# First batch of the last attention, begun inside the feed-forward

## Chip, cores, metric

One core of one Trainium2 chip. The metric is the device time of the whole kernel in microseconds (us), lower is better.

## What is computed

A two-layer stack on x of shape (4, 512, 256), with a context of (4, 64, 256). All data are fp32.

```python
x = x + xattn0(layernorm(x), ctx)      # 12 heads of 64, layernorms of q and k
x = x + ffn0(layernorm(x))
x = x + xattn1(layernorm(x), ctx, mask)  # 16 heads of 16, 64 keys, masked softmax
x = x + moe(layernorm(x))              # 8 experts, top 1

def ffn0(x):   # 256 -> 1024 -> 1024 -> 1024 -> 256, ternary weights, scales per output
    h = silu((x @ w1.T) * s1) * ((x @ w2.T) * s2)
    h = gelu((h @ h1.T) * t1)
    h = gelu((h @ h2.T) * t2)
    return (h @ w3.T) * s3

def xattn1(q, k, v, mask):
    scores = (q @ Wq.T + bq) . (k @ Wk.T + bk) / 4, where(mask == 0, -1e9)
    return softmax(scores) . (v @ Wv.T + bv) @ Wo.T + bo
```

## The kernel before

The core runs four stages in a row: first attention, feed-forward, last attention, experts. Each of the first three loops over the four batches of 512 tokens (four token tiles of 128). The program for each engine is written out by hand, in the order in which its instructions stand, and semaphores tie the engines together. An engine that waits holds everything that stands behind the wait in its own program. PSUM has eight banks of 128 x 512 fp32: the feed-forward turns through banks 2 to 7 (`ring_bank`, L1086), banks 0 and 1 are for transposes, queries, probabilities and heads.

**Feed-forward** (`ffn_tensor` L1158, `ffn_scalar` L1249, `ffn_vector` L1264, `ffn_gpsimd` L1140). The hidden values are kept transposed, 128 hidden units by 512 tokens, as a rounded part and a remainder (`f_ha`, `f_hb`: `hi` and `lo`), since the ternary weights are exact in the one-pass form of fp32. So each product is a sum of matmuls for `hi` and for `lo`. Per batch there are four layers. The first has eight columns of two products each (`fw1`, `fw2`): ScalarE takes Silu of the one into `f_raw`, VectorE multiplies it by the other (L1273), rounds it (L1279) and takes the remainder (L1280). The second (`fh1`) and third (`fh2`) have eight products of 16 matmuls of 128x512, ScalarE takes Gelu, VectorE splits the result in the same way. `f_raw` has three buffers, so ScalarE waits for the split of three results before. The fourth layer (`fw3`) gives four token products, one for each token tile, of 16 matmuls of 256 columns. Its first two are issued as a pair. VectorE's end of a token tile (from L1292) is: product times scale into `f_tmp`, sum with the residual, moments, variance plus epsilon.

In batch 0, VectorE also checks the bits of the weights of the third and fourth layers, between the first and the second layer's splits (L1281), and sends TensorE a flag (`take_bits`, `f_checked`); TensorE reads it before the last product of the second layer. Both forms of every product stand in the program, behind a branch, and the one-pass form is what runs with these weights.

**Last attention** (`attn1_tensor` L1528, `attn1_scalar` L1688, `attn1_vector` L1777, `attn1_gpsimd` L1434, `attn1_sync` L1364). For batch b: columns are the transposed normalised tokens (`attn1_columns` L1303, copied out by ScalarE, L1338); queries are their product with `Wq` (L1331, copied out with scale and bias, L1343); both go through banks 0 and 1. Keys are spread over head blocks by GpSimd (`attn1_keys` L1423). The scores of a token tile (L1543, L1547) are ten matmuls into two banks, 2 and 3 or 4 and 5 in turn. VectorE takes the maximum over each head's 64 keys and subtracts it (L1787, L1788), ScalarE takes the exponential, VectorE the sum and its reciprocal (L1796, L1797), GpSimd divides (L1456). TensorE transposes the probabilities (L1562), multiplies them by the values (`heads`, L1572), projects (L1586). The gate part (L1318) is a product of the columns with the experts' gate weights, and `fold` (L1595, L1599) folds `Wo` and its bias into the gate weights, once.

Before the change, the first batch's columns and queries stand in the feed-forward's third layer of the last batch (after its fourth and sixth product, L1231 to L1235), and everything else of the attention stands behind the feed-forward. TensorE's order for batch b of the attention (L1643): scores of tiles 0 and 1, gate part, columns of batch b+1, queries of batch b+1, scores of tile 2, scores of tile 3, with the transposes, heads and projections of earlier batches between them; batch 0 has `fold` last. Scores of tile n in all wait for the subtraction two tiles before. SyncE loads the second-layer weights of all experts (8 MB, `ew2`) after the first batch's fourth scores (L1367).

## Time and profile before

| | us |
|---|---|
| median of three runs | 800.45 |
| lowest, highest | 796.26, 801.01 |
| the profiled execution | 798.0 |
| span of its instructions | 796.1 |
| TensorE busy in the span | 745.0 |
| VectorE busy | 460.0 |
| ScalarE busy | 248.4 |
| GpSimd busy | 183.4 |

The profile shows one execution. PE is TensorE, DVE is VectorE, ACT is ScalarE, POOL is GpSimd, SP is SyncE. PEclk is the granted clock of TensorE as a share of full speed. A timeline's row is a run of equal instructions: its start, its length, and in brackets how long the engine stood idle before it and on whom it waited.

### The profile page before, as it was taken

To read this page: it belongs to the slowest core of one execution; us is meant where nothing else is said; L and a number is where in the kernel's file an instruction comes from. 1 tells how busy PE (TensorE), PEld (TensorE's weight loads), DVE (VectorE), ACT (ScalarE), POOL (GpSimd) and SP (SyncE) were. 2 spreads that over 40 slices of the span, in tenths; PEclk is the share of its full clock that TensorE was granted. 3 is DMA by queue.
4 is the path that set the end of the run, shared out by engine and by line. 5 is a ranking of instruction groups with operands and counts; after the bars stand their busy time and mean duration, and the time that the engine had idled before them with its cause. 6 is when DMAs were issued, how large, how long until landed. Compare 5 with 4: busy or idle time off the path is not lost.

```text
span 796.1 us, 11304 instructions
## 1 busy us (share of the span) xinstructions
PE 745.0 (94%) x4168; PEld 578.6 (73%) x4168; DVE 460.0 (58%) x897; ACT 248.4 (31%) x455; POOL 183.4 (23%) x183
## 2 busy tenths in 40 slices
PE   5999899989999999999999999998987699999995
PEld 3676576768878888888888888775554597777674
DVE  4646479888982584348424943289798742333331
ACT  3425133132311132123222321256566232223221
POOL 3012134461020002000200020056564222222221
PEclk9979999999999999999999999999999899999998
DMA  9970800002300000000000000019013878899950
GB/s 326 383 254 2 369 1 0 1 1 80 134 2 2 2 2 2 2 2 2 2 2 2 2 2 2 2 25 412 1 54 107 275 268 312 259 282 302 310 159 7
DMA packets 21726, 86.64 MB, mean 109 GB/s; under 512 B 3229, under 2 KB 12384, under 8 KB 16352
## 3 DMA queue, kind: packets, MB, share of 16 engines
q1 hardware_dynamic: 19088, 78.18, 27.8%
q0 software_dynamic: 2560, 7.34, 2.7%
q8 instruction: 59, 0.97, 0.5%
q14 instruction: 19, 0.16, 0.1%
HBM read 79.22 MB, written 18.35 MB: 123 GB/s over the span
## 4 chain that ended last, share of the span: by engine, by line
PE 79%; DVE 13%; issue 4%; DMA 1%; ACT 1%; POOL 1%; SPq 0%; DVEq 0%; POOLq 0%
PE ps L1178 37%; PE ps L2177 8%; PE ps L2150 6%; PE ps L593 5%; PE ps L544 4%; PE ps L2142 3%; PE ps L1331 2%; PE ps L530 2%; DVE any_bits L357 2%; DVE head_max L1787 1%; PE ps L622 1%; DVE head_sum L1796 1%; PE ps L538 1%; DMA xs<-rows,token_in 1%; PE ps L1543 1%
## 5 line engine op out<-in xcount | busy, mean ns | idle before, releaser
L1256 ACT ACTIVATE f_raw<-ps,cols 128x512 f32<-128x512 f32 x96 | 66.2, 690 | 242.1 <-PE ps L1178 219.4
L1178 PE MATMUL ps<-f_ha_hi,fh 128*128 128x512 f32 x256 | 99.9, 390 | 1.6 <-DVE inexact L377 1.5
L1178 PE MATMUL ps<-f_hb_hi,fh 128*128 128x512 f32 x256 | 100.1, 391 | 0.0
L1178 PE MATMUL ps<-f_ha_lo,fh 128*128 128x512 f32 x256 | 99.6, 389 | 0.0
L1178 PE MATMUL ps<-f_hb_lo,fh 128*128 128x512 f32 x256 | 99.6, 389 | 0.0
L1279 DVE CAST f_ha_hi<-f_raw 128x512 fp32r<-128x512 f32 x64 | 27.6, 432 | 84.9 <-ACT f_raw L1256 83.9
L2177 PE MATMUL ps<-ew,hT 128*128 (+1 forms) x320 | 72.7, 381 | 2.3 <-ACT hT L2230 1.8
L2177 PEld LDWEIGHTS ps<-ew,hT 128*128 128x128 f32 (+1 forms) x320 | 52.5, 169 | 16.5 <-issue 4.4
L1178 PEld LDWEIGHTS ps<-f_ha_hi,fh 128*128 128x128 f32 x256 | 48.1, 188 | 12.3 <-issue 2.4
L1178 PEld LDWEIGHTS ps<-f_hb_lo,fh 128*128 128x128 f32 x256 | 48.1, 188 | 10.2 <-issue 0.2
L1178 PEld LDWEIGHTS ps<-f_hb_hi,fh 128*128 128x128 f32 x256 | 48.1, 188 | 10.2 <-issue 0.2
L1178 PEld LDWEIGHTS ps<-f_ha_lo,fh 128*128 128x128 f32 x256 | 48.1, 188 | 9.9
L2150 PE MATMUL ps<-xsT,ew 128*128 128x128 f32 (+1 forms) x416 | 50.4, 281 | 1.5 <-DVE xsT L2019 1.5
L2150 PEld LDWEIGHTS ps<-xsT,ew 128*128 128x128 f32 x416 | 49.6, 197 | 2.6 <-DVE xsT L2019 2.1
L544 PE MATMUL ps<-m_all,a_xT 128*128 128x384 f32 x128 | 48.9, 530 | 2.0 <-DVE a_tok L920 2.0
L1178 PE MATMUL ps<-f_xT_hi,fw 128*128 128x512 f32 x128 | 50.0, 391 | 0.0
L1178 PE MATMUL ps<-f_xT_lo,fw 128*128 128x512 f32 x128 | 49.9, 389 | 0.0
L1279 DVE CAST f_hb_hi<-f_raw 128x512 fp32r<-128x512 f32 x32 | 17.9, 558 | 51.8 <-ACT f_raw L1256 51.8
L1280 DVE TENSOR_TENSOR f_ha_lo<-f_raw,f_ha_hi 128x512 fp32r<-128x512 f32 x64 | 44.6, 697 | 2.2
L593 PE MATMUL ps<-vw_all,a_pT 128*128 128x256 f32 x192 | 43.7, 381 | 0.6 <-DVE x_res L946 0.5
L1082 POOL TENSOR_TENSOR rstd_all<-var_eps,const 128x4 f32<-128x4 f32 x4 | 4.1, 1037 | 171.9 <-DVE var_eps L338 171.9
L593 PEld LDWEIGHTS ps<-vw_all,a_pT 128*128 128x128 f32 x192 | 35.8, 190 | 7.2 <-issue 1.0
(322 smaller groups left out, 1362.3 us busy)
## 6 DMA issues: line engine op xcount, KB each, us to landing
ew<-in_ew SPq DMA_DIRECT2D x27, 1028.0 KB, 6.8
fh<-fh_copy SPq DMA_DIRECT2D x2, 4096.0 KB, 14.9
ew<-in_ew SPq DMA_DIRECT2D x1, 8192.0 KB, 22.3
b_rows<-in_eb SPq DMA_DIRECT2D x14, 256.0 KB
fw<-fw_copy SPq DMA_DIRECT2D x3, 1024.0 KB, 6.9
x_res<-in_x SPq DMA_DIRECT2D x4, 512.0 KB, 10.6
rows<-x_res SPq DMA_DIRECT2D x4, 512.0 KB, 3.5
rows<-xn_e SPq DMA_DIRECT2D x4, 512.0 KB, 3.0
```

The costliest lines, as they stand in the source:

```text
L357: order.step(nc.vector.tensor_tensor(bits[:], so_far, piece, ALU.bitwise_or))
L530: ins = nc.tensor.matmul(ps[:, c, :], gram[:, k, c * P:(c + 1) * P], a_xT[:, k, :], start=(k == 0), stop=(k == KD - 1))
L544: ins = nc.tensor.matmul(ps[:, 2 + 2 * (j % 2) + h, 0:HALF], a_xT[:, k, j * P:(j + 1) * P], m_all[:, b, k, h * HALF:(h + 1) * HALF], start ...
L593: ins = nc.tensor.matmul(ps[:, 7 - j % 2, 0:D], a_pT[:, g, j * P:(j + 1) * P], vw_all[:, b, g, :], start=(g == 0), stop=(g == PAIRS - 1))
L1178: ins = nc.tensor.matmul(out, *((xk, wk) if swap else (wk, xk)), start=(k == 0 and part == 0), stop=(k == w.shape[1] - 1 and part == 1))
L1256: nc.scalar.activation(f_raw[:, m % 3, :], ps[:, ring_bank(n), :], ACT.Silu if m < KH else ACT.Gelu, scale=col(("w1_s", "h1_s", "h2_s")[m ...
L1279: order.step(nc.vector.tensor_copy(hi, raw))
L1280: nc.vector.tensor_tensor(lo, raw, hi.bitcast(F32), ALU.subtract).then_inc(f_split, 1)
L1331: ins = nc.tensor.matmul(ps[:, o, :], wq1[:, k, o * P:(o + 1) * P], first_or(c_xT, b)[:, k, :], start=(k == 0), stop=(k == KD - 1))
L2142: ins = nc.tensor.matmul(bank[half_rows(h), :], xsT[:, t % 2, k, half_rows(h)], ew1[n % LOAD_RING][:, at_:at_ + 4 * P], start=(k == 0), st ...
L2150: ins = nc.tensor.matmul(bank[:, q * P + part.start:q * P + part.stop], ew1[loads[0] % LOAD_RING][:, at_:at_ + P], xsT[:, t % 2, k, part], ...
L2177: ins = nc.tensor.matmul(ps[part, 6 + t % 2, 0:D], hT[:, t % 2, k, part], ew2[:, bass.ts(e, 1), k, :].rearrange("p a n -> p (a n)"), start ...
```

## The change

The last batch's columns and queries of the first attention batch move from the third to the second layer of the feed-forward. Its keys (own tile `k_first`) are made when the second layer's products are done. Its scores (into banks 0 and 1) and their maxima, subtractions, exponentials and sums go in between the token products of the fourth layer and the end of the feed-forward, with an own tile `c_first`. Both tiles lie where the second layer's weights were, which is also where `ew2` goes, so its load now waits for the first batch's probability transposes. And in the first layer of every batch the rounding of the gated value moves from VectorE to ScalarE (`gated_high`), with the remainder taken by VectorE one column later (`gated_low`).

```diff
+        def score_bank(b, j):
+            return 0 if b == 0 else 2 + 2 * (j % 2)
...
-                        if w is fh2 and i == LAST and o == 3:
+                        if w is fh1 and i == LAST and o == KH - 3:
                             after(pe, f_in, B, 2, 2)
                             attn1_columns(pe, 0)
-                        if w is fh2 and i == LAST and o == 5:
+                        if w is fh1 and i == LAST and o == KH - 1:
                             attn1_queries(pe, 0)
...
                 for j in range(2, TT):
+                    if i == LAST:
+                        attn1_scores(pe, 0, j - 2)
                     ring_free(pe, i, 4 * KH + j)
                     product(second, ps[:, ring_bank(4 * KH + j), 0:D], fw3, f_ha, slice(0, D), tokens[j],
                             f_mm_full, swap=True)
+                if i == LAST:
+                    attn1_scores(pe, 0, 2)
+                    attn1_scores(pe, 0, 3)
+
+        def gated_high(act, i, o):
+            after(act, f_up_taken, i, KH, o + 1)
+            nc.scalar.activation(f_ha[0][:, o, :], f_raw[:, o % 3, :], ACT.Identity).then_inc(f_hi, 1)
...
+                def gated_low(o):
+                    dve.wait_ge(f_hi, i * KH + o + 1)
+                    nc.vector.tensor_tensor(f_ha[1][:, o, :], f_raw[:, o % 3, :], f_ha[0][:, o, :].bitcast(F32),
+                                            ALU.subtract).then_inc(f_split, 1)
...
-                        after(dve, f_up_taken, i, KH, o + 1)
+                        if o:
+                            gated_low(o - 1)
+                        if o == KH - 1:
+                            gated_low(o)
...
                     add_eps(j).then_inc(f_var, 1)
+                    if i == LAST:
+                        attn1_subtract_max(dve, s_order, 0, j)
+                if i == LAST:
+                    for j in range(TT):
+                        attn1_invert_sum(dve, s_order, 0, j)
...
+        def attn1_scores(pe, b, j):
+            n = b * TT + j
+            if j == 0:
+                pe.wait_ge(c_q_out, NG1 * (b + 1))
+                pe.wait_ge(c_keys, NG1 * (b + 1))
+            if b == 0:
+                if j:
+                    pe.wait_ge(c_sub, j)
...
-            sp.wait_ge(c_s_full, 1)
+            after(sp, f_mm_full, LAST, F_MM, 4 * KH)
             sp.dma_start(wo1n[:], wo1n_d).then_inc(ld_fold, 16)
-            sp.wait_ge(c_s_full, TT)
+            sp.wait_ge(c_pT_full, PAIRS1)
             sp.dma_start(ew2[:], ew2_d.rearrange("e p k n -> p e k n")).then_inc(ld_ew, 16)
...
-            if b == 0:
-                after(pool, f_mm_full, LAST, F_MM, 4 * KH)
-            if b >= 2:
+            if b < 2:
+                after(pool, f_mm_full, LAST, F_MM, (3 + b) * KH)
+            else:
                 pool.wait_ge(c_s_full, TT * (b - 1))
...
             for b in range(B):
-                scores(b, 0)
-                scores(b, 1)
+                if b == 0:
+                    pe.wait_ge(c_sub, TT)
+                else:
+                    attn1_scores(pe, b, 0)
+                    attn1_scores(pe, b, 1)
                 gate_part(pe, b)
...
+            exponential(0, 0)
+            exponential(0, 1)
             rows_in(1)
+            exponential(0, 2)
+            exponential(0, 3)
```

How the order of instructions moves, on TensorE from the end of the fourth layer's last token product to the second batch. L1178 is the token product, L1543 and L1547 the scores, L1318 the gate part, L1310 columns, L1331 queries, L1595 and L1599 the fold; `c_qT_123` are the first batch's queries, `c_qT_125` the second's. Before:

```order
L1178 MATMUL ps<-fw_78,f_ha_hi 128x256
L1178 MATMUL ps<-fw_78,f_ha_lo 128x256
L1170 UNCONDITIONAL_BRANCH
L1543 MATMUL ps<-k_blocks,c_qT_123 128x256 x4
L1547 MATMUL ps<-each_key,fillT 128x512 x2
L1543 MATMUL ps<-k_blocks,c_qT_123 128x256 x4
L1547 MATMUL ps<-each_key,fillT 128x512 x2
L1318 MATMUL ps<-c_xT_121,gate_w 32x128 x8
L1310 MATMUL ps<-const,x_in 128x128 x8
L1331 MATMUL ps<-c_xT_122,wq_69 128x512 x4
L1543 MATMUL ps<-k_blocks,c_qT_123 128x256 x4
L1547 MATMUL ps<-each_key,fillT 128x512 x2
```
After (token product L1191, scores L1360 and L1364, gate part L1402, columns L1394, queries L1415, fold L1658 and L1662; `k_first` are the first batch's keys):

```order
L1191 MATMUL ps<-fw_78,f_ha_hi 128x256
L1191 MATMUL ps<-fw_78,f_ha_lo 128x256
L1183 UNCONDITIONAL_BRANCH
L1360 MATMUL ps<-k_first,c_qT_125 128x256 x4
L1364 MATMUL ps<-each_key,fillT 128x512 x2
L1360 MATMUL ps<-k_first,c_qT_125 128x256 x4
L1364 MATMUL ps<-each_key,fillT 128x512 x2
L1402 MATMUL ps<-c_xT_123,gate_w 32x128 x8
L1394 MATMUL ps<-const,x_in 128x128 x8
L1415 MATMUL ps<-c_xT_124,wq_69 128x512 x4
L1658 MATMUL ps<-gate_w,wo1n 128x8 x4
L1662 MATMUL ps<-gate_w,const 128x8 x2
```
The four scores of the first batch that stood around the second batch's columns and queries now stand ahead of them all (two of them further up, between the token products), and the fold stands right behind the queries.

On VectorE, from the last token tile's end to the second batch's maxima (L1292 to L338 the tile end, L1787 and L1788 maximum and subtraction, L1796 and L1797 sum and reciprocal). Before:

```order
L1292 TENSOR_TENSOR f_tmp<-ps,rows 128x256
L1297 TENSOR_TENSOR x_res<-x_res,f_tmp 128x256
L324 BN_STATS stats<-x_res 128x6
L327 BN_AGGR mean_var<-stats 128x2
L338 TENSOR_SCALAR var_eps<-mean_var 128x1
L1787 TENSOR_REDUCE head_max<-ps 128x16
L1788 TENSOR_TENSOR c_tok_118<-ps,head_max 128x1024
L1787 TENSOR_REDUCE head_max<-ps 128x16
L1788 TENSOR_TENSOR c_tok_118<-ps,head_max 128x1024
L1796 TENSOR_REDUCE head_sum<-c_tok_118 128x16
L1797 RECIPROCAL head_sum<-head_sum 128x16
L1787 TENSOR_REDUCE head_max<-ps 128x16
```
After (the tile end L1327 to L340, maximum and subtraction L1375 and L1376, sum and reciprocal L1384 and L1385):

```order
L1327 TENSOR_TENSOR f_tmp<-ps,rows 128x256
L1332 TENSOR_TENSOR x_res<-x_res,f_tmp 128x256
L326 BN_STATS stats<-x_res 128x6
L329 BN_AGGR mean_var<-stats 128x2
L340 TENSOR_SCALAR var_eps<-mean_var 128x1
L1375 TENSOR_REDUCE head_max<-ps 128x16
L1376 TENSOR_TENSOR c_first<-ps,head_max 128x1024
L1384 TENSOR_REDUCE head_sum<-c_first 128x16
L1385 RECIPROCAL head_sum<-head_sum 128x16
L1384 TENSOR_REDUCE head_sum<-c_first 128x16
L1385 RECIPROCAL head_sum<-head_sum 128x16
L1384 TENSOR_REDUCE head_sum<-c_first 128x16
```
Each tile end is now followed by its tile's maximum and subtraction, and the four sums stand together behind the last of them.

## Rows read from the trace of the kernel before

**Rows 1.** The page: granted clock in 40 slices, and the costliest TensorE group of L1178.

```profile
PEclk9979999999999999999999999999999899999998
...
L1178 PE MATMUL ps<-f_ha_hi,fh 128*128 128x512 f32 x256 | 99.9, 390 | 1.6 <-DVE inexact L377 1.5
```
**Rows 2.** Timeline of TensorE, 524 to 550 us: start, length, what, idle before.

```profile
524.28 0.28 PE L1178 MATMUL ps<-fw,f_ha_hi 128*128 128x256 f32 x1
524.40 0.28 PE L1178 MATMUL ps<-fw,f_ha_lo 128*128 128x256 f32 x1
524.62 1.13 PE L1543 MATMUL ps<-k_blocks,c_qT 64*128 64x256 f32 x8
...
526.97 0.64 PE L1318 MATMUL ps<-c_xT,gate_w 128*32 128x128 f32 x16
...
529.38 3.70 PE L1331 MATMUL ps<-c_xT,wq 128*128 128x512 f32 x8 [0.71 <-ACT c_xT L1338]
533.01 1.13 PE L1543 MATMUL ps<-k_blocks,c_qT 64*128 64x256 f32 x8
...
535.37 1.06 PE L1595 MATMUL ps<-gate_w,wo1n 128*128 128x8 f32 x8
...
537.25 1.14 PE L1543 MATMUL ps<-k_blocks,c_qT 64*128 64x256 f32 x8
...
540.68 1.14 PE L1543 MATMUL ps<-k_blocks,c_qT 64*128 64x256 f32 x8 [2.08 <-DVE c_tok L1788]
...
542.07 1.08 PE L1318 MATMUL ps<-c_xT,gate_w 128*32 128x128 f32 x16
...
545.73 3.70 PE L1331 MATMUL ps<-c_xT,wq 128*128 128x512 f32 x8 [0.69 <-ACT c_xT L1338]
549.37 1.13 PE L1543 MATMUL ps<-k_blocks,c_qT 64*128 64x256 f32 x8
```
**Rows 3.** Timeline of VectorE, 520 to 551 us.

```profile
520.41 0.42 DVE L1292 TENSOR_TENSOR f_tmp<-ps,rows 128x256 f32<-128x256 f32 x1 [0.82 <-PE ps L1178]
...
527.60 1.22 DVE L1787 TENSOR_REDUCE head_max<-ps 128x16 f32<-128x1024 f32 x1
...
529.99 1.22 DVE L1787 TENSOR_REDUCE head_max<-ps 128x16 f32<-128x1024 f32 x1
...
540.55 1.21 DVE L1796 TENSOR_REDUCE head_sum<-c_tok 128x16 f32<-128x1024 f32 x1
...
541.96 1.16 DVE L1796 TENSOR_REDUCE head_sum<-c_tok 128x16 f32<-128x1024 f32 x1
...
543.33 1.16 DVE L1787 TENSOR_REDUCE head_max<-ps 128x16 f32<-128x1024 f32 x1
...
550.75 1.23 DVE L1787 TENSOR_REDUCE head_max<-ps 128x16 f32<-128x1024 f32 x1 [1.21 <-PE ps L1547]
```
**Rows 4.** Timeline of GpSimd: the first batch's first division.

```profile
533.96 1.90 POOL L1456 TENSOR_TENSOR c_tok<-c_tok,head_sum 128x1024 f32<-128x1024 f32 x1
```
**Rows 5.** Windows: length, busy time of each engine (instructions), granted clock, DMA share, GB/s.

```profile
542.00:543.00 1.00, 1.00 (x18) 0.59 (x16) 1.00 (x2) 0.00 (x0) 0.88 (x1) 0.50 1.02 434
624.00:626.00 2.00, 0.00 (x0) 0.00 (x0) 1.35 (x8) 0.98 (x2) 1.65 (x4) 0.50 1.07 393
630.00:631.00 1.00, 1.00 (x8) 1.00 (x8) 0.86 (x7) 0.00 (x0) 0.00 (x0) 0.72 0.90 194
```
**Rows 6.** Gated values: the page's group of casts, timelines of ScalarE and TensorE in batch 0.

```profile
L1279 DVE CAST f_ha_hi<-f_raw 128x512 fp32r<-128x512 f32 x64 | 27.6, 432 | 84.9 <-ACT f_raw L1256 83.9
...
197.13 0.69 ACT L1256 ACTIVATE f_raw<-ps,cols 128x512 f32<-128x512 f32 x1 [1.15 <-PE ps L1178]
...
236.41 0.49 PE L1178 MATMUL ps<-f_ha_hi,fh 128*128 128x512 f32 x1 [1.50 <-DVE inexact L377]
```
**Rows 7.** The load of expert weights (page), and their first use (chain of waits).

```profile
ew<-in_ew SPq DMA_DIRECT2D x1, 8192.0 KB, 22.3
...
638.60 3.46 PE ps L2177 x16
```

More of the change, by code:

```diff
@@ L1299, in ffn_vector @@
                     add_eps(j).then_inc(f_var, 1)
-                order.end()
+                    if i == LAST:
[3 more added lines that the diff above has]
+                        attn1_invert_sum(dve, s_order, 0, j)
+                order.end()
+        def attn1_scores(pe, b, j):
[6 more added lines that the diff above has]
+                    pe.wait_ge(c_sub, j)
+            elif n == TT:
+                after(pe, f_act_out, LAST, F_HID, F_HID)
+            elif n == TT + 1:
+                after(pe, f_y_taken, LAST, TT, TT - 1 + 2)
+            else:
+                pe.wait_ge(c_sub, n - 1)
+            halves = [(ps[:, score_bank(b, j) + r, :], slice(r * KEYS, (r + 1) * KEYS)) for r in range(2)]
+            for o in range(NG1):
+                for bank, half in halves:
+                    nc.tensor.matmul(bank[:, o * D:(o + 1) * D], first_or(c_qT, b)[half, o, j * P:(j + 1) * P],
+                                     keys_of(b)[half, o].rearrange("p g k -> p (g k)"),
+                                     start=(o == 0), stop=False)
+            for bank, half in halves:
+                ins = nc.tensor.matmul(bank, fillT[half, j * P:(j + 1) * P],
+                                       each_key[half].rearrange("p g k -> p (g k)"), start=False, stop=True)
+            ins.then_inc(c_s_full, 1)
@@ new lines, in attn1_subtract_max @@
+        def attn1_subtract_max(dve, order, b, j):
+            dve.wait_ge(c_s_full, TT * b + j + 1)
+            if b >= 2:
+                dve.wait_ge(c_pT_full, PAIRS1 * (b - 1))
+            first = score_bank(b, j)
+            logits = ps[:, first:first + 2, :].rearrange("p o (g k) -> p (o g) k", k=KEYS)
+            top_ = head_max[:, j, :]
+            order.step(nc.vector.tensor_reduce(top_, logits, AX.X, ALU.max))
+            nc.vector.tensor_tensor(tokens_of(b)[:, j], logits, top_.unsqueeze(2).broadcast_to([P, H1, KEYS]),
+                                    ALU.subtract).then_inc(c_sub, 1)
@@ L1303, in attn1_columns, with attn1_invert_sum @@
+        def attn1_invert_sum(dve, order, b, j):
+            dve.wait_ge(c_exp, TT * b + j + 1)
+            if b:
+                dve.wait_ge(c_prob, TT * (b - 1) + j + 1)
+            sums = head_sum[:, j, :]
+            order.step(nc.vector.tensor_reduce(sums, tokens_of(b)[:, j], AX.X, ALU.add))
+            nc.vector.reciprocal(sums, sums).then_inc(c_inv, 1)
         def attn1_columns(pe, b):
@@ L1592, in fold @@
                 pe.wait_ge(consts_ready, 1)
+                after(pe, f_y_taken, LAST, TT, 2 * TT - 1)
                 for m in range(KD):
@@ L1653, in attn1_tensor @@
                     attn1_queries(pe, b + 1)
-                scores(b, 2)
-                if b >= 1:
-                    probabilities(b - 1, 0, 2)
-                scores(b, 3)
                 if b == 0:
                     fold()
-                if b >= 1:
+                else:
+                    attn1_scores(pe, b, 2)
+                    probabilities(b - 1, 0, 2)
+                    attn1_scores(pe, b, 3)
                     probabilities(b - 1, 2, 2)
@@ L1690, in exponential @@
                 act.wait_ge(c_sub, TT * b + j + 1)
[L1691 removed]
+                nc.scalar.activation(tokens_of(b)[:, j], tokens_of(b)[:, j], ACT.Exp).then_inc(c_exp, 1)
             def rows_in(b):
@@ L1730, in attn1_scalar @@
                     attn1_columns_out(act, b + 1)
-                exponential(b, 0)
-                exponential(b, 1)
+                if b:
+                    exponential(b, 0)
+                    exponential(b, 1)
                 if b < LAST:
@@ L1845, in logits, with subtract_max, invert_sum @@
                 g_order.step(nc.vector.tensor_tensor(e, raw, by_expert(row("gate_b", E), TT), ALU.add))
-            for b in range(B):
+            def subtract_max(b, j):
+                attn1_subtract_max(dve, s_order, b, j)
+            def invert_sum(b, j):
+                attn1_invert_sum(dve, s_order, b, j)
+            for b in range(1, B):
                 subtract_max(b, 0)
```

87 lines of the change are left out of this document (30 added, 57 removed).

## The prediction

> **What bounds the kernel now.** I read the page first: the granted clock of TensorE is full or nearly so in all but three of 40 slices, and its costliest group, 256 matmuls of the feed-forward, has 1.6 us of idle time before it in all [rows 1]. So the feed-forward is TensorE's alone, and columns and queries that move from one of its layers to another neither fill nor open a hole. What the change can win or lose lies in the passage from the feed-forward to the last attention (520 to 550 us), and in whatever the new split of the gated values touches.
>
> Passage, timeline of TensorE [rows 2]: the first batch's scores start at 524.62, its gate part at 526.97, the second batch's queries at 529.38, scores of token tile 2 at 533.01, the folded gate products at 535.37, the second batch's first scores at 537.25. Then a wait of 2.08 us for VectorE's subtraction, the second scores at 540.68, gate part 542.07, queries 545.73, tile 2 at 549.37. TensorE works ahead of VectorE and is stopped by it once.
>
> Passage, timeline of VectorE [rows 3]: from 520.41 it has hardly a pause. A tile end (product times scale, sum, moments, epsilon) takes (527.60 - 520.41) / 4 = 1.80 us, a maximum with its subtraction 529.99 - 527.60 = 2.39, a sum with its reciprocal 541.96 - 540.55 = 1.41. Four of each are 4 x 5.60 = 22.4 us; 520.41 + 22.4 = 542.8, and the second batch's first maximum starts at 543.33. There is 0.5 us of slack: the passage is VectorE's, and moving its work about behind the same first product (520.4) can't bring in more than that.
>
> **The change part by part.** (a) The path of VectorE. It now does tile end, maximum and subtraction tile by tile, 1.80 + 2.39 = 4.19 us each. The first maximum needs scores that TensorE issues behind the first two token products. The last two are 32 matmuls, 0.12 us apart, that end at 524.6 [rows 2], so the first two end at 520.8; two scores take 2.35 us there, one about 1.2, so the maximum can start near 522.1, just when VectorE ends its first tile end (522.2). The subtractions end at 522.2 + 2.48 + 4.19 j: 524.7, 528.9, 533.1, 537.3; then come four sums until 542.9. VectorE loses nothing and gains 0.5.
>
> (b) The path of TensorE. The first batch's scores share one pair of banks (0 and 1), and each waits for the subtraction before it: waits of about 0.8, 1.0 and 3.0 us. Ahead of the gate part stands a new wait for the fourth subtraction, 3 us more, since columns and queries write banks 0 and 1 too. Behind it on TensorE are queued gate part, columns and queries of the second batch, the folded products and two scores. In the kernel before, most of these ran while VectorE took its maxima; now nothing of them does. At full clock, from [rows 2]: gate part to queries 529.38 - 526.97 = 2.41 (plus 0.3, since ScalarE first does the fourth exponential), queries 533.01 - 529.38 = 3.63, fold 537.25 - 535.37 = 1.88, two scores 526.97 - 524.62 = 2.35. From 537.35 that gives 547.9 for the second gate part, which started at 542.07. From a gate part to the scores of tile 2 it is 533.01 - 526.97 = 6.04: 553.95 against 549.37, 4.6 us late. VectorE is done at 542.9 and waits until about 547 for the second batch's first scores. That is the new wait, and it is longer than the one removed.
>
> Does the delay survive? The maximum of tile 2 at 550.75 waited 1.21 us for exactly these scores [rows 3], and transposes, heads and the next batch's scores follow from it in a chain; I see no place where 4 us could be regained. GpSimd starts its first division at 533.96, 6.4 us after the last tile end [rows 4]; that end moves to 534.8, so the first division starts near 541.1 and the fourth, at 1.90 each, ends near 548.8. The transposes that need it come after 555. It is covered, and if the cover went, each us past 555 would cost one.
>
> (c) The clock. It is half (1.2 of 2.4 GHz) in the window 542 to 543 [rows 5], behind the wait of 2.08 us, and by 545.73 the queries had their full price again (549.37 - 545.73 = 3.64). Idle in 624 to 626, TensorE had half clock too, and the full one came back within 630 to 631 [rows 5]. The half clock shows in the same pieces: gate part to queries 545.73 - 542.07 = 3.66 instead of 2.41. In the changed kernel TensorE has about 1.2 us of work between 530.1 and 537.35, so I expect half clock there, ending 4 to 5 us into the dense work, as in both rows. Gate part to queries then takes 3.66 instead of 2.41 + 0.3: +0.95; about 1 us of the queries falls under it: +0.5. The slow spell of the kernel before (549.37 - 542.07 = 7.30, against 6.04) is gone, and that is in (b) already. Bounds: 0 (no fall) and +3.2 (slow until 545). I take +1.45. (b) and (c) make +6.05 us.
>
> The Trainium skill, "TensorE: Matmul & The Clock Gate", section "HAM oscillation — how this bites in real kernels", says that an engine that waits between bursts of work can fall to the cold clock and begin each burst cold. By that rule the whole chain behind the fourth subtraction could run at half clock; the fall at 542 agrees with it, no row here shows it repeated burst by burst, and its outcome is rival B.
>
> (d) Gated values. In the first layer, 8 casts of 0.43 us a batch leave VectorE for ScalarE. There an activation takes 0.69 us and waits 1.15 us for the next product [rows 6], room for one more. In the later batches TensorE shows no wait that this could shorten: nothing. In batch 0, behind the last gated split, VectorE checks bits of the weights and then catches up before it delivers the flag by which TensorE picks the form of the third and fourth layers' products; TensorE waits 1.50 us for that flag [rows 6]. 8 x 0.43 = 3.4 us less, of which about 1 is lost to waiting for products, should bring the flag before TensorE asks for it. Bounds 0 and -1.5; I take -1.5, since 2.4 is well over 1.5.
>
> (e) Moved and cheap. Columns and queries of the first batch are the same matmuls, one layer earlier; their normalised tokens must be there, and GpSimd makes them right after the first split of the second layer's output, four products ahead of the columns. The first batch's keys move to an earlier idle time of GpSimd. The 8 MB load of expert weights now waits for the first batch's transposes, some 28 us later, near 563; at 22.3 us to landing it is there near 586, and the second expert layer reads it at 638.60 [rows 7]. 50 us of cover. The row stores behind it on SyncE's queue wait for later work anyhow. Cost 0; were it late, TensorE would stand at its first such product.
>
> **Sum.** +6.05 - 1.5 = +4.5 us on a profiled execution of 798.0 us (span 796.1 and 1.9 around it): 802.5. The three runs before have a median of 800.45 (796.26 to 801.01), so the forecast for the median is 800.45 + 4.5 = 805.0.
>
> **The rivals.** A, the forecast: +3 to +7. B, slower by over 1%: the clock does not come back. Between waits and narrow matmuls it stays at half through queries (+3.6), fold (up to +1.9) and two scores (542.07 - 540.68 = 1.39 against 1.18, +0.4): 4.6 + 0.95 + 3.6 + 1.9 + 0.4 - 1.5 = +10, 810.4. For it: seven sparse us ahead of the chain. Against it: in both rows the clock was back 5 us after work resumed. It decides if the clock is still at half after 545. C, not slower: VectorE stays the bound. Were TensorE's chain from the fourth subtraction to the second batch's first scores shorter than VectorE's four sums (5.6 us), VectorE would run through, and 0.5 and 1.5 us would be won: 798.5. For it speaks that TensorE stood waiting in the passage before; against it that the chain adds up to 2.7 + 3.6 + 1.9 + 1.2 = 9.4 us with nothing beside it. D: as A, but the flag of batch 0 comes no earlier, because the catching up behind it hangs on ScalarE and GpSimd as much as on VectorE's start: +6, 806.5.
>
> **How the numbers follow.** A 0.62, B 0.13, C 0.10, D 0.15. A measurement of this kernel tells about 1%, 8 us, from no change. Slower by over 8 us: most of B and a little of A and D, 0.14. Faster by over 8 us: no case reaches it, 0.03 for what I have not seen. Within: 0.83. The range is 799 to 810 and leaves out the far ends of B and C; the spread of the three runs, 5 us, is as wide as the terms in dispute.
>
> **What would show it.** TensorE: a wait of about 3 us before the fourth scores, and another before the gate part, which starts near 536 (the whole passage lies 1.5 us earlier by batch 0). VectorE: a wait of 4 to 6 us for scores between the fourth reciprocal and the second batch's first maximum. Clock: half speed somewhere between 532 and 542. Batch 0: the wait for the flag under 0.3 us. It is wrong if VectorE runs from 520 to 547 without a pause, if the second gate part starts before 545, or if TensorE waits for the expert weights.

## The result, and the profile after

| | before | after |
|---|---|---|
| median, us | 796.47 (21 runs, 794.07 to 801.01) | 801.85 (21 runs, 800.10 to 807.37) |
| span of the profiled execution | 796.1 | 799.9 |
| TensorE, VectorE, ScalarE, GpSimd busy | 745.0, 460.0, 248.4, 183.4 | 744.6, 446.3, 265.7, 183.1 |

The ratio is 1.0065, with a 95% interval of 1.005 to 1.0081: slower by about 5.2 us (the two medians lie 5.4 us apart), and within 1%. The forecast was +4.5 us. Its absolute figure, 805.0, is 3 us above the measured one: it was built on the three runs then at hand (800.45), and over 21 runs the median of before is 796.47, 4 us less. From that median the same +4.5 us would have given 801.0.

VectorE does 14 us less and ScalarE 17 us more (the casts have moved), TensorE does the same work. So the loss is idle time, and the place has to be found. First a warning about subtraction. The spans differ by 3.8 us, less than the timed difference, since the two profiled executions already differ before any changed instruction: in 40 to 60 us, in the first attention, the granted clock was 0.74 in the kernel before and 0.91 in the kernel after, and the feed-forward's first product started at 193.98 and at 191.32. I therefore count from the feed-forward's first product, and from its fourth layer's first token product.

The page of the kernel after, for [rows 1 and 7]:

```profile
PEclk9999999999999999999999999979999899999998
...
L1191 PE MATMUL ps<-f_ha_hi,fh 128*128 128x512 f32 x256 | 99.8, 390 | 0.0
...
ew<-in_ew SPq DMA_DIRECT2D x1, 8192.0 KB, 23.7
```
The third digit, the early one, is now 9. There is a new 7 in the slice from 520 to 540 us, the passage between feed-forward and attention. The 1.6 us before the feed-forward's products are gone: that was the flag's wait.

The timeline of TensorE after (start, length, what, idle before and on whom it waited), for [rows 2 and 6]:

```profile
191.32 0.58 PE L1191 MATMUL ps<-f_xT_hi,fw 128*128 128x512 f32 x1
...
512.02 0.28 PE L1191 MATMUL ps<-fw,f_ha_hi 128*128 128x256 f32 x1
...
519.91 1.13 PE L1360 MATMUL ps<-k_first,c_qT 64*128 64x256 f32 x8 [0.52 <-DVE c_first L1376]
...
524.10 1.13 PE L1360 MATMUL ps<-k_first,c_qT 64*128 64x256 f32 x8 [0.73 <-DVE c_first L1376]
...
528.28 1.97 PE L1360 MATMUL ps<-k_first,c_qT 64*128 64x256 f32 x8 [2.84 <-DVE c_first L1376]
...
533.26 1.08 PE L1402 MATMUL ps<-c_xT,gate_w 128*32 128x128 f32 x16 [2.58 <-DVE c_first L1376]
...
536.92 6.25 PE L1415 MATMUL ps<-c_xT,wq 128*128 128x512 f32 x8 [0.69 <-ACT c_xT L1422]
543.01 0.95 PE L1658 MATMUL ps<-gate_w,wo1n 128*128 128x8 f32 x8
...
544.78 1.14 PE L1360 MATMUL ps<-k_blocks,c_qT 64*128 64x256 f32 x8
...
547.14 0.64 PE L1402 MATMUL ps<-c_xT,gate_w 128*32 128x128 f32 x16
...
549.55 3.70 PE L1415 MATMUL ps<-c_xT,wq 128*128 128x512 f32 x8 [0.70 <-ACT c_xT L1422]
553.18 1.14 PE L1360 MATMUL ps<-k_blocks,c_qT 64*128 64x256 f32 x8
```
The four waits for subtractions are there, the last one (2.58 us) ahead of the gate part. Behind it the queries take 6.25 us; eight equal matmuls take 3.70 us at 549.55. Between the last wait and the second gate part, 533.26 to 547.14, lie 13.88 us.

The timeline of VectorE after, for [rows 3]:

```profile
515.58 0.42 DVE L1327 TENSOR_TENSOR f_tmp<-ps,rows 128x256 f32<-128x256 f32 x1 [1.12 <-PE ps L1191]
...
530.72 1.22 DVE L1375 TENSOR_REDUCE head_max<-ps 128x16 f32<-128x1024 f32 x1 [0.70 <-PE ps L1364]
...
538.46 0.25 DVE L1385 RECIPROCAL head_sum<-head_sum 128x16 f32<-128x16 f32 x1
546.17 1.23 DVE L1375 TENSOR_REDUCE head_max<-ps 128x16 f32<-128x1024 f32 x1 [7.46 <-PE ps L1364]
...
554.57 1.22 DVE L1375 TENSOR_REDUCE head_max<-ps 128x16 f32<-128x1024 f32 x1 [2.11 <-PE ps L1364]
```
From the first tile end to the end of the last reciprocal (538.46 + 0.25 = 538.71) VectorE is as quick as it was: 538.71 - 515.58 = 23.1 us, against 22.9 in the kernel before, from the first tile end to the second batch's first maximum (520.41 to 543.33). Then it stands idle for 7.46 us until TensorE delivers the second batch's first scores. That hole is the loss.

The timeline of GpSimd after, for [rows 4]:

```profile
535.04 0.40 POOL L1559 COPY bo_wide<-cols 128x256 f32<-128x256 f32 x1
...
536.11 7.47 POOL L1540 TENSOR_TENSOR c_first<-c_first,head_sum 128x1024 f32<-128x1024 f32 x4
```
The first division comes 6.1 us behind the last tile end (530.02), against 6.4 before, and the fourth ends at 543.6; the transposes that read them start only at 554.46. It is covered.

Windows after (length, busy time of each engine with instructions, granted clock, DMA share, GB/s), for [rows 5]:

```profile
526.00:528.00 2.00, 0.00 (x0) 0.00 (x0) 1.97 (x2) 1.10 (x3) 0.00 (x0) 1.00 0.00 0
528.00:530.00 2.00, 1.72 (x8) 1.23 (x10) 1.73 (x6) 1.06 (x1) 0.00 (x0) 0.61 0.00 0
530.00:532.00 2.00, 0.68 (x4) 0.00 (x0) 1.27 (x3) 0.00 (x0) 1.66 (x5) 0.50 0.00 0
...
540.00:542.00 2.00, 2.00 (x3) 0.67 (x2) 0.00 (x0) 0.69 (x1) 2.00 (x2) 0.50 0.00 0
542.00:544.00 2.00, 2.00 (x13) 1.37 (x11) 0.00 (x0) 0.79 (x2) 2.00 (x2) 0.98 0.04 8
```
TensorE is idle in 526 to 528 with the full clock still granted. Half clock (1.2 GHz) begins near 528.4, just as the fourth scores start, and full clock (2.4 GHz) is back at 542, nearly 9 us after the dense work began at 533.26.

### The profile page after: what moved, and what is told of

Its sections match the earlier page's. It is cut to its first block, busy times and chain, and to the rows that moved or that the text cites. A ratio compares the mean times of both kernels' runs of the same rounds, so it can differ in the third digit from the quotient of the medians.

```text
span 799.9 us, 11304 instructions
## 1 busy us (share of the span) xinstructions
PE 744.6 (93%) x4168; PEld 577.3 (72%) x4168; DVE 446.3 (56%) x865; ACT 265.7 (33%) x487; POOL 183.1 (23%) x183
## 4 chain that ended last, share of the span: by engine, by line
PE 81%; DVE 10%; issue 3%; DMA 2%; ACT 1%; POOL 1%; SPq 0%; DVEq 0%; POOLq 0%
PE ps L1191 40%; PE ps L2233 8%; PE ps L2206 6%; PE ps L595 5%; PE ps L546 4%; PE ps L2198 3%; PE ps L1415 2%; PE ps L532 2%; DVE head_max L1375 2%; PE ps L624 1%; DVE head_sum L1384 1%; DMA xs<-rows,token_in 1%; PE ps L1360 1%; PE ps L540 1%; PE ps L648 1%
## 5 line engine op out<-in xcount | busy, mean ns | idle before, releaser
L1191 PE MATMUL ps<-f_hb_hi,fh 128*128 128x512 f32 x256 | 100.0, 391 | 0.0
L1191 PE MATMUL ps<-f_ha_hi,fh 128*128 128x512 f32 x256 | 99.8, 390 | 0.0
L1191 PE MATMUL ps<-f_ha_lo,fh 128*128 128x512 f32 x256 | 99.6, 389 | 0.0
L1191 PE MATMUL ps<-f_hb_lo,fh 128*128 128x512 f32 x256 | 99.6, 389 | 0.0
L1314 DVE CAST f_ha_hi<-f_raw 128x512 fp32r<-128x512 f32 x32 | 14.0, 437 | 82.6 <-ACT f_raw L1280 82.6
L1191 PEld LDWEIGHTS ps<-f_hb_lo,fh 128*128 128x128 f32 x256 | 48.1, 188 | 10.2 <-issue 0.2
L1191 PEld LDWEIGHTS ps<-f_hb_hi,fh 128*128 128x128 f32 x256 | 48.1, 188 | 10.2 <-issue 0.2
L1191 PEld LDWEIGHTS ps<-f_ha_lo,fh 128*128 128x128 f32 x256 | 48.1, 188 | 9.9
L1191 PEld LDWEIGHTS ps<-f_ha_hi,fh 128*128 128x128 f32 x256 | 48.1, 188 | 9.9
L1191 PE MATMUL ps<-f_xT_hi,fw 128*128 128x512 f32 x128 | 50.0, 391 | 0.0
L1191 PE MATMUL ps<-f_xT_lo,fw 128*128 128x512 f32 x128 | 49.9, 389 | 0.0
L546 PE MATMUL ps<-m_all,a_xT 128*128 128x384 f32 x128 | 46.3, 508 | 2.0 <-DVE a_tok L922 2.0
L2104 DVE TENSOR_TENSOR ys<-ps,eb 128x256 f32<-128x256 f32 (+1 forms) x20 | 8.5, 424 | 52.9 <-PE ps L2233 33.8
## 6 DMA issues: line engine op xcount, KB each, us to landing
ew<-in_ew SPq DMA_DIRECT2D x1, 8192.0 KB, 23.7
```

The lines of the kernel that those rows point to most:

```text
L546: ins = nc.tensor.matmul(ps[:, 2 + 2 * (j % 2) + h, 0:HALF], a_xT[:, k, j * P:(j + 1) * P], m_all[:, b, k, h * HALF:(h + 1) * HALF], start ...
L1191: ins = nc.tensor.matmul(out, *((xk, wk) if swap else (wk, xk)), start=(k == 0 and part == 0), stop=(k == w.shape[1] - 1 and part == 1))
L1314: order.step(nc.vector.tensor_copy(hi, raw))
L2104: nc.vector.tensor_tensor(ys[part, u, :], ps[part, 6 + t % 2, 0:D], eb2[part, u, :], ALU.add)\
```

## The experiments

Theory 1 is the forecast: VectorE starves because gate part, columns, queries, fold and two scores now stand behind the wait for the fourth subtraction, partly under half clock. Rivals: the gated values or the moved columns, queries and load cost something; or the loss is the clock alone; or the order of VectorE's work in the passage is bad in itself, whatever the banks. Seven kernels were made to tell these apart, in two batches, each with its own runs of the kernel before: median 796.36 over 24 runs for gated_alone, without_gated, scores_in_ring and filled_waits, 796.21 over 26 for moved_alone, ring_early_bias and all_scores_first. The medians of the seven are over 12 runs each, but 9 of all_scores_first, 7 of without_gated and 6 of scores_in_ring; those of before and after in the table are over 21. "To token" is the time from the feed-forward's first product to its first token product in the last batch, "to tile 2" the time from that same first product to the second batch's scores of tile 2, both in us, from TensorE's timeline of one profiled execution each.

| kernel | median, us | ratio to before (95%) | to token | to tile 2 |
|---|---|---|---|---|
| before | 796.47 | 1 | 322.87 | 355.39 |
| after | 801.85 | 1.0065 (1.005 to 1.0081) | 320.70 | 361.86 |
| gated_alone | 795.77 | 0.9986 (0.9964 to 1.0008) | 320.68 | 354.25 |
| without_gated | 802.80 | 1.0079 (1.005 to 1.0108) | 322.87 | 364.38 |
| moved_alone | 796.02 | 0.9975 (0.9954 to 0.9995) | 320.65 | 355.87 |
| filled_waits | 799.72 | 1.0033 (1.0013 to 1.0054) | 320.66 | 357.41 |
| scores_in_ring | 806.67 | 1.0115 (1.0078 to 1.0152) | 320.67 | 362.94 |
| ring_early_bias | 797.55 | 1.0012 (0.999 to 1.0033) | 320.66 | 354.99 |
| all_scores_first | 792.37 | 0.9951 (0.9929 to 0.9973) | 320.66 | 350.72 |

### The gated values, alone and taken out

gated_alone is the kernel before with nothing but the new split of the gated values:

```diff
+        def gated_high(act, i, o):
+            after(act, f_up_taken, i, KH, o + 1)
+            nc.scalar.activation(f_ha[0][:, o, :], f_raw[:, o % 3, :], ACT.Identity).then_inc(f_hi, 1)
...
+                        if o:
+                            gated_low(o - 1)
+                        if o == KH - 1:
+                            gated_low(o)
```


> The kernel before with only the gated values changed (rounding on ScalarE, remainder one column later). My theory: batch 0's flag comes before TensorE asks for it, its wait of 1.50 us goes, all else stays: 1.5 us less than before, ratio 0.998, and from the feed-forward's first product to its last 1.6 us less. Rival (the flag is not what held TensorE, or ScalarE becomes late): no change or slower, ratio 1.000 or more.

without_gated is the kernel after with the old split:

```diff
-                        if o:
-                            gated_low(o - 1)
-                        if o == KH - 1:
-                            gated_low(o)
+                        after(dve, f_up_taken, i, KH, o + 1)
...
+                    hi, lo = (part[:, o, :] for part in (f_hb if m // KH == 1 else f_ha))
+                    order.step(nc.vector.tensor_copy(hi, raw))
+                    nc.vector.tensor_tensor(lo, raw, hi.bitcast(F32), ALU.subtract).then_inc(f_split, 1)
```


> The changed kernel with the gated values as they were before. My theory: the passage's loss stays alone, 1.5 us more than the changed kernel, ratio to before 1.0085, and batch 0's wait of 1.5 us is there again. Rival (the parts are tied to each other): the same as the changed kernel, 1.0065.

In the traces the effect is plain. Every kernel with the new split has 320.65 to 320.70 us to its first token product, the two without it 322.87: 2.2 us. The flag's wait stands in TensorE's timeline of without_gated, and in that of no kernel with the new split:

```profile
231.85 0.49 PE L1189 MATMUL ps<-f_ha_hi,fh 128*128 128x512 f32 x1 [1.49 <-DVE inexact L379]
```
In the timed runs it is smaller than the noise: 0.9986 alone, 1.0065 against 1.0079 within the change; both point the same way, but the one interval reaches over 1 and the other overlaps with the change's. Part of it is also given back at once: gated_alone is 2.19 us ahead at the token products and 1.14 at tile 2, mostly since its second scores, which wait for VectorE's subtraction, ran at half clock (2.08 us where the kernel before has 1.14 at 540.68 [rows 2]). So this part of the change is a small gain in place, and cannot be the loss.

### The moves, without the interleaving

moved_alone is gated_alone with the first batch's columns and queries in the second layer and the late load of `ew2`, but with scores, maxima and keys where they were:

```diff
-                        if w is fh2 and i == LAST and o == 3:
+                        if w is fh1 and i == LAST and o == KH - 3:
...
-                        if w is fh2 and i == LAST and o == 5:
+                        if w is fh1 and i == LAST and o == KH - 1:
...
-            sp.wait_ge(c_s_full, TT)
+            sp.wait_ge(c_pT_full, PAIRS1)
```


> The kernel gated_alone, with the first batch's columns and queries in the second layer of the feed-forward and the load of expert weights behind the first batch's probability transposes; scores and maxima as before. Theory: both moves cost nothing, ratio equal to that of gated_alone within its interval, 0.997 to 1.000; TensorE never waits for the expert weights. Rival (the late load meets the row stores or the first expert products): over 1.002.

It measured 0.9975 (0.9954 to 0.9995), and 320.65 us to the token products, as gated_alone. The moves show no cost in the timed runs. At tile 2 its profiled execution is 1.62 us behind that of gated_alone (355.87 against 354.25), and TensorE's timeline shows that this is the clock:

```profile
534.91 2.08 PE L1561 MATMUL ps<-k_blocks,c_qT 64*128 64x256 f32 x8 [2.09 <-DVE c_tok L1806]
...
541.01 5.35 PE L1349 MATMUL ps<-c_xT,wq 128*128 128x512 f32 x8 [0.69 <-ACT c_xT L1356]
```
The queries took 5.35 us where the kernel before and gated_alone have 3.70. All three kernels have the same order of TensorE's work here, and the same wait of 2.08 or 2.09 us for the subtraction. Yet full clock was back 4.5 us behind that wait in the kernel before, 5.5 us in gated_alone and 9.5 us in moved_alone. So the length of such a spell is not fixed by the order of the work, and one execution can't price it to better than a us or two.

With the moves and the gated values ruled out, all of the loss is in the interleaved scores and maxima (with their earlier keys).

### The clock

filled_waits is the kernel after with 12 matmuls of 128x512 ahead of each of the last two waits; their results go to a bank where nothing reads them:

```diff
+        def keep_busy(pe, n):
+            after(pe, f_act_out, LAST, F_HID, F_HID)
+            for _ in range(n):
+                nc.tensor.matmul(ps[:, 2, :], fw3[:, 0, 0:P].bitcast(F32R), f_ha[0][:, 0, :], start=True, stop=True)
...
+                if j == 3:
+                    keep_busy(pe, 12)
...
+                    keep_busy(pe, 12)
                     pe.wait_ge(c_sub, TT)
```


> The changed kernel with 12 extra matmuls of 128x512 into the idle bank 2 ahead of each of the last two waits for VectorE (before the fourth scores and before the gate part); their results are not used. They fit in the waits of 2.8 and 2.6 us. My theory: the clock stays full, queries take 3.7 instead of 6.25 us, and 3 us of the loss go: ratio to before 1.003. Rival (the chain alone is the loss, the clock only what a profile happens to show): within 1 us of the changed kernel, ratio 1.0055 to 1.0075.

It measured 1.0033 where the change has 1.0065, and the two intervals only just touch: half of the loss goes, half stays. The two fillings end within 0.2 us of the subtractions, so they hold up little. Its window:

```profile
526.00:538.00 12.00, 11.31 (x63) 7.12 (x62) 11.02 (x17) 4.78 (x8) 8.09 (x17) 1.00 0.00 1
```
and its timeline of TensorE:

```profile
532.18 0.64 PE L1409 MATMUL ps<-c_xT,gate_w 128*32 128x128 f32 x16
...
534.64 3.70 PE L1422 MATMUL ps<-c_xT,wq 128*128 128x512 f32 x8 [0.69 <-ACT c_xT L1429]
...
542.32 0.65 PE L1409 MATMUL ps<-c_xT,gate_w 128*32 128x128 f32 x16
...
558.19 3.28 PE L1641 MATMUL ps<-c_pT,v_blocks 128*32 128x512 f32 x16 [1.84 <-ACT c_pT L1785]
```
With the clock full, first to second gate part takes 542.32 - 532.18 = 10.14 us instead of 13.88. Up to tile 2 the kernel is 361.86 - 357.41 = 4.45 us better than the change, which is what half clock cost there in these two executions. That they are no exceptions is seen from the timed runs: the granted clock, averaged over the span, was 0.984 to 0.987 in all 12 runs of filled_waits and 0.975 to 0.981 in all 21 of the kernel after. Part of the gain was lost again later: after a pause of 1.84 us, which the kernels before and after have too, a new half-clock spell made the heads at 558.19 take 3.28 us, where the kernels before and after have 1.92. VectorE still waits 3.85 us for the second batch's first scores:

```profile
541.35 1.23 DVE L1382 TENSOR_REDUCE head_max<-ps 128x16 f32<-128x1024 f32 x1 [3.85 <-PE ps L1371]
```
So the clock alone is not the cause; the chain behind the wait is there at full clock too.

### Taking the shared banks away

scores_in_ring gives the first batch's scores the ring's banks, as the other batches', leaves only tile 0's scores between the token products, and puts the other three where they stood before the change. The exponentials go back with them. The gate part then waits for nobody:

```diff
         def score_bank(b, j):
-            return 0 if b == 0 else 2 + 2 * (j % 2)
+            return 2 + 2 * (j % 2)
...
-                    if i == LAST:
-                        attn1_scores(pe, 0, j - 2)
+                    if i == LAST and j == 2:
+                        attn1_scores(pe, 0, 0)
...
-                if b == 0:
-                    pe.wait_ge(c_sub, TT)
-                else:
+                if b:
                     attn1_scores(pe, b, 0)
-                    attn1_scores(pe, b, 1)
+                attn1_scores(pe, b, 1)
                 gate_part(pe, b)
```


> The changed kernel, but the first batch's scores go into banks 2 to 5 in turn as before, only tile 0's scores stand between the token products, and gate part, columns and queries of the second batch stand ahead of the scores of tiles 2 and 3 again, with no wait for the fourth subtraction. VectorE's order is that of the changed kernel. My theory (the loss is the chain behind the new wait): the loss goes and VectorE runs from 520 on with no pause over 1 us, second gate part about 3 us earlier than in the kernel before; 2 to 4 us less than before, ratio 0.995 to 0.998. Rival (VectorE's interleaved order, or the late load of expert weights, costs the time): still slower than before, ratio over 1.003.

This expectation failed outright: 1.0115, worse than the change. TensorE's timeline shows where:

```profile
523.03 0.64 PE L1396 MATMUL ps<-c_xT,gate_w 128*32 128x128 f32 x16
...
540.25 1.85 PE L1652 MATMUL ps<-gate_w,wo1n 128*128 128x8 f32 x8 [8.75 <-POOL bo_wide L1553]
...
543.73 2.08 PE L1354 MATMUL ps<-k_blocks,c_qT 64*128 64x256 f32 x8
```
The gate part did move up, from 21.2 us behind the first token product to 10.5. But the fold then waited 8.75 us for GpSimd, and everything behind it with it. GpSimd's timeline tells why:

```profile
534.88 1.04 POOL L1084 TENSOR_TENSOR rstd_all<-var_eps,const 128x4 f32<-128x4 f32 x1 [20.91 <-DVE var_eps L340]
...
539.74 0.41 POOL L1553 COPY bo_wide<-cols 128x256 f32<-128x256 f32 x1
```
It sat idle for 20.91 us in front of the last tile end and only then, as the seventh of its jobs, copied the bias out. The interleaving makes the last tile end late, so the copy is late. In the kernel after this is hidden, since the fold starts at 543.01 and the copy at 535.04. VectorE waits too:

```profile
523.14 1.22 DVE L1369 TENSOR_REDUCE head_max<-ps 128x16 f32<-128x1024 f32 x1 [0.98 <-PE ps L1358]
...
530.46 1.23 DVE L1369 TENSOR_REDUCE head_max<-ps 128x16 f32<-128x1024 f32 x1 [3.04 <-PE ps L1358]
...
546.27 1.22 DVE L1369 TENSOR_REDUCE head_max<-ps 128x16 f32<-128x1024 f32 x1 [3.64 <-PE ps L1358]
```
The scores of tile 1 stand behind all token products, those of tile 2 behind gate part, columns and queries. So two causes were on offer for the bad time, GpSimd's copy and the order of the scores, and one experiment was made for each.

ring_early_bias is scores_in_ring with the copy right behind the second batch's keys, in front of the long wait:

```diff
                     attn1_keys(pool, 1)
+                    pool.tensor_copy(bo1_wide[:], cols[:, COLS["bo1"]:COLS["bo1"] + KD].unsqueeze(2)
+                                     .broadcast_to([P, KD, P])).then_inc(consts_ready, 1)
                 after(pool, f_var, i, TT, TT)
```


> The kernel scores_in_ring, with one move: GpSimd spreads the bias for the fold right behind the second batch's keys, not behind its chores after the last tile end. There TensorE stood 8.75 us before the fold for that tile, with the second batch's scores queued behind. Theory: that wait goes, no pause over 1 us before the fold, the second batch's first scores start at VectorE's third subtraction, and VectorE runs from its sums into the second batch's first maximum; its earlier waits of 1.0 and 3.0 us for scores stay, so the time is near that of the kernel before: ratio 0.997 to 1.001. Rival (the loss of scores_in_ring was in VectorE's order or in the clock): still over 1.007.

It measured 1.0012 where scores_in_ring has 1.0115, each kernel against its batch's own runs of before: one copy of 0.4 us, moved, was worth 1% of the kernel. GpSimd's timeline:

```profile
511.79 0.60 POOL L1161 COPY bo_wide<-cols 128x256 f32<-128x256 f32 x1
532.77 1.04 POOL L1084 TENSOR_TENSOR rstd_all<-var_eps,const 128x4 f32<-128x4 f32 x1 [20.38 <-DVE var_eps L340]
```
VectorE's waits for the scores of tiles 1 and 2 (0.99 and 3.04 us) are still there, so it is no faster than before. all_scores_first takes these as well: tiles 0 and 1 between the token products, tiles 2 and 3 right behind the last one and ahead of gate part, columns and queries, and the third exponential earlier. Its edit of TensorE's program, against ring_early_bias:

```diff
-                    if i == LAST and j == 2:
-                        attn1_scores(pe, 0, 0)
+                    if i == LAST:
+                        attn1_scores(pe, 0, j - 2)
...
-                attn1_scores(pe, b, 1)
+                    attn1_scores(pe, b, 1)
+                else:
+                    attn1_scores(pe, b, 2)
+                    attn1_scores(pe, b, 3)
                 gate_part(pe, b)
```


> The kernel ring_early_bias, with the first batch's scores of tiles 0 and 1 between the token products and those of tiles 2 and 3 right behind the last one, ahead of gate part, columns and queries; four banks in turn, so that no score waits long for a subtraction; ScalarE takes the third exponential ahead of the third batch's rows. Theory: VectorE has no wait over 0.3 us from the first tile end to the maximum of the second batch's tile 2, which starts about 28.6 us after the first tile end, against 30.3 in the kernel before; with the gated values' 1.5 us the time is 3 to 4 us under the kernel before: ratio 0.995 to 0.9965. Rival (what is won at the start is lost to GpSimd's divisions, which end later than before): ratio 0.998 to 1.000.

TensorE's order in the passage is now that of the kernel after: both have these scores ahead of gate part and queries. Against the kernel after three things differ. The scores take four banks in turn, and nothing else of TensorE's waits for the fourth subtraction. GpSimd's copy is early. And ScalarE's exponentials stand behind its copies of the second batch's gate part and columns, which in the kernel after waited for the fourth exponential, and by it for the fourth subtraction.

It measured 0.9951 (0.9929 to 0.9973), 792.37 us, faster than the kernel before and over 9 us below the kernel after. VectorE's timeline:

```profile
519.35 0.42 DVE L1326 TENSOR_TENSOR f_tmp<-ps,rows 128x256 f32<-128x256 f32 x1 [1.04 <-PE ps L1193]
...
541.89 1.16 DVE L1371 TENSOR_REDUCE head_max<-ps 128x16 f32<-128x1024 f32 x1
...
548.02 1.16 DVE L1371 TENSOR_REDUCE head_max<-ps 128x16 f32<-128x1024 f32 x1
```
From the first tile end to the second batch's first maximum it has 22.5 us (22.9 before, 30.6 after), and to that batch's third maximum 28.7 (30.3 before, 39.0 after), and none of the rows in between has a wait in brackets. TensorE's timeline:

```profile
524.01 1.13 PE L1356 MATMUL ps<-k_first,c_qT 64*128 64x256 f32 x8 [0.85 <-DVE f_tmp L1326]
...
529.74 0.64 PE L1398 MATMUL ps<-c_xT,gate_w 128*32 128x128 f32 x16
...
532.15 3.70 PE L1411 MATMUL ps<-c_xT,wq 128*128 128x512 f32 x8 [0.71 <-ACT c_xT L1418]
```
Its windows, granted clock third from the end:

```profile
520.00:540.00 20.00, 18.45 (x148) 13.32 (x150) 18.73 (x32) 9.24 (x14) 5.82 (x15) 1.00 0.01 2
540.00:560.00 20.00, 15.09 (x108) 8.71 (x102) 16.70 (x20) 14.22 (x26) 19.33 (x14) 1.00 0.16 53
```
One short wait for a bank is left, the clock is full through the whole passage, and tile 2 comes 4.7 us earlier than in the kernel before: 2.2 of them from the gated values, and about 1.3 since the half-clock spell of the kernel before (7.30 against 6.04 us from gate part to tile 2) isn't there. VectorE's order is the same as in the kernel after, so that rival is refuted. What differs is who waits: with four banks in turn the scores run ahead of VectorE's maxima, and nothing else of TensorE's is held by a subtraction. What the banks, the early copy and the later exponentials are worth each was not measured on the kernel after.

## Why the prediction was right, and where it was off

**What bounds the kernel, and (a), VectorE's path: right.** The passage was VectorE's; its own work between the first tile end and the last sum took 23.1 us, forecast 22.5. The 0.6 us more are the 0.70 us wait for the fourth scores, which ran at half clock (1.97 us where the third took 1.13).

**(b), TensorE's chain behind the new wait: right, in kind and size.** Counted from the first token product, tile 2 came at 32.52 us in the kernel before. At full clock the forecast put it 4.6 us later; filled_waits, which has the clock full there, has it at 548.35 - 511.60 = 36.75, 4.23 later. The waits of TensorE were forecast as 0.8, 1.0, 3.0 and 3 us and are 0.52, 0.73, 2.84 and 2.58. The wait of VectorE was forecast as 4 to 6 us and is 7.46 with half clock and 3.85 without.

**(c), the clock: right in kind, too small by two thirds.** +1.45 was taken, with +3.2 as bound. Measured, after against filled_waits from the first token product to tile 2: 41.16 - 36.75 = 4.41 us. The failed step is "ending 4 to 5 us into the dense work, as in both rows": it ended nearly 9 us in. The two rows were too few to take a length from: moved_alone, with the order of the kernel before in this passage, had full clock back only 9.5 us behind its wait. Of the 4.41 us, 0.66 lie ahead of the gate part (the fourth scores), 1.20 between gate part and queries (3.66, as forecast, against 2.46), and 2.55 in the queries (6.09 against 3.54), for which the forecast had put +0.5. Fold and two scores (1.77 and 2.36 us) ran at full clock again.

What made the spell so long is not shown. Between the waits TensorE had less work than in the kernel before (busy 13.17 of 20 us in 520 to 540, against 17.89), and two of its waits (2.84 and 2.58 us) were longer than the one of 2.08 us; no run takes these apart. without_gated, which has the same passage, shows the same: half clock from 529.1 to 542.8, and 41.51 us from the first token product to tile 2, against 41.16. The Trainium skill, "TensorE: Matmul & The Clock Gate", section "HAM oscillation — how this bites in real kernels", describes a kernel whose bursts begin cold after each wait. This trace agrees only in part: the burst behind the wait at 533.26 did run at 1.2 GHz, but the fourth scores behind the wait of 2.84 us began at full clock, which fell within 0.2 us, and full clock was back for the second half of the dense work.

**(d), the gated values: right, 2.17 us in the trace against 1.5.** The flag's wait of 1.50 went, and with it a gap of 0.28 us of batch 0 where the second layer begins, which the forecast did not count; the remaining 0.4 us lie in pieces too small to be placed. As a time of the whole kernel it is not told from nothing.

**(e), the moves: right.** moved_alone is no slower than the kernel before. In the kernel after the load of expert weights is issued at 561.20 and lands 23.7 us later, near 585 (forecast: 563 and 586), and the second expert layer's first product at 641.83 waits for nothing.

**Does the delay survive: right, in full.** From the second batch's tile 2 to the first expert product it is 78.09 us before (549.37 to 627.46) and 78.07 after (553.18 to 631.25), and from there to the end 168.6 in both. The sum for the profiled executions is -2.17 + 4.23 + 4.41 = +6.47 at tile 2 (355.39 to 361.86); the forecast's was +4.5, and the timed runs say +5.2. The over 1 us between trace and timed runs is not explained by any run. One reason may be that the profiled execution of before had the shortest half-clock spell of the three kernels with its order. That the forecast came so near the timed figure is in part luck: at tile 2 it was 2 us short, since the clock cost 3 us more than it said and (b) and (d) together 1 us less.

**The rivals.** B had the clock staying at half through queries, fold and scores, +10. It was half right: most of the queries were slow, but not what stands behind them. Its test (half clock after 545) came out on the line: 545 is 28 to 30 us behind the forecast's first token product, and the half clock ended 30 us behind the measured one; but the price was 4.4 us for the clock, where B needed 7. C is refuted by the idle 7.46 us, D by the missing wait for the flag. That GpSimd was covered held for the kernel after, with over 7 us to spare at the fold. But the forecast had looked at GpSimd's divisions alone, and scores_in_ring showed that the copy for the fold is the nearer one.

**Open.** Why full clock is back 4.5 us behind a wait in one execution and 9 us behind it in another, and why half clock comes at all at 558 in filled_waits, is not settled by these runs. The early half-clock spell in the first attention differs between executions and was not studied.

## What to carry to other kernels

When a step of an in-order engine is made to wait for another engine, price what is queued behind that wait, not the wait: here 2.58 us of waiting for a bank held 10 to 14 us of TensorE's work that the bounding engine needed. Interleaving stages pays if the producer has buffers enough to run ahead of the consumer, and if it gives the bounding engine's inputs first. For the buffers: the same order on TensorE with four banks instead of two, the copy early and the exponentials later went from +0.65% to -0.5%. For the order: with four banks and the early copy, the scores of tiles 2 and 3 behind gate part and queries gave +0.1%, ahead of them -0.5%. And when an event moves late, look through the quiet engines for small jobs that stand behind it in program order: one copy of 0.4 us on an engine idle for 20 us made a difference of 1%.

## What the runs showed of the hardware

Half clock has no fixed length, not even for one order of work. Around the same wait of 2.1 us it lasted about 3 us in the kernel before (541.8 to 545.2), 7 in gated_alone (533.4 to 540.2) and 10 in moved_alone (534.1 to 544.4), read from the granted clock in windows of 0.5 us. It also fell at different points: 1.1 us after work had begun again in the first, still within the wait in the other two. In the kernel after it lasted nearly 14 (528.4 to 542.1). In gated_alone another spell stands among the experts. Its window:

```profile
660.00:680.00 20.00, 18.25 (x99) 13.70 (x98) 6.10 (x11) 3.54 (x10) 3.98 (x4) 0.91 0.75 228
```
There a group of 16 matmuls took 5.40 us, where a like group of the kernel after took 3.71. Such spells differ from execution to execution, and so one profiled span doesn't order the kernels as the timed runs do: all_scores_first has the best median, but its profiled execution was the slowest of its nine (797.96 us, span 796.1), while gated_alone has a span of 793.8. Of this, 5 us arose before the feed-forward, which began at 195.14 in the one and 190.19 in the other, with a granted clock of 0.74 and 0.91 in 40 to 60 us.

Filling waits with unused matmuls did raise the clock (0.71 to 1.00 in 520 to 540), and bought 2.6 us of the 5.2. Taking the waits away, so that TensorE did its real work in that time, bought over 9.

ScalarE took 32 more casts of 128x512 (17 us of busy time in all) in the first layers, and no product of TensorE came later for it: all seven kernels with the new split reach the token products 2.2 us earlier than the two without.
